# A Swin block on one core: K, Q and V as three fp16 products each, the loop written out, fc2 rows ahead of the first transposes

## The reference

```python
y = roll(ln(x, norm1_g, norm1_b), (-3, -3))        # then cut into 8 x 8 windows of 49 pixels
q, k, v = heads(yw @ qkv_w.T + qkv_b)              # 16 heads of 8 channels
attn = softmax(q * 8**-0.5 @ k.T + bias + mask)    # 49 x 49 for each window and head
o = roll(windows_back((attn @ v) @ proj_w.T + proj_b), (3, 3))
x = x + o
h = gelu(ln(x, norm2_g, norm2_b) @ fc1_w.T + fc1_b)   # 512 hidden channels
return x + (h @ fc2_w.T + fc2_b)
```

## Time and profile before

| | before |
|---|---|
| median of 3 runs | 4402.2 us (4398.3 to 4403.4) |
| the profiled execution | 4409.2 us, its span 4407.4 us |
| PE busy | 4134.3 us, 94% |
| weight loads (PEld) | 3265.2 us, 74% |
| DVE busy | 2743.0 us, 62% |
| ACT busy | 2889.0 us, 66% |
| POOL busy | 2014.4 us, 46% |
| mean granted TensorE clock | 0.983 of the upper level |
| row maxima, DVE line 576 | 1024 of 975 ns |
| exp, ACT line 418 | 1024 of 822 ns |
| K and Q, PE line 816 | 1024 records (two for each fp32 product) |
| V, PE line 850 | 4096 records |
| transfers | 443 MB, the 16 DMA engines 34% busy |

### The profile page before, as it was taken

One profiled execution on the slowest core, in us unless ns is written; L12 is line 12 of the kernel. 1 busy time (PEld: TensorE's weight loads), 2 busy tenths in 40 slices (PEclk: granted clock), 3 DMA queues, 4 the chain that ended last, 5 costly groups with the idle time before them and its releaser, 6 DMA issues.

```text
span 4407.4 us, 179808 instructions
## 1 busy us (share of the span) xinstructions
PE 4134.3 (94%) x72586; PEld 3265.2 (74%) x72586; DVE 2743.0 (62%) x6930; ACT 2889.0 (66%) x5120; POOL 2014.4 (46%) x3472
## 2 busy tenths in 40 slices
PE   3999999999999999999999999999999999999998
PEld 2777777777777777777777777777777777777777
DVE  5666665666656656566565656666566566666663
ACT  2666666666666666666666666766666666666665
POOL 4444444444444444444444444444444444444443
PEclk8999999999999999999999999999999999999999
DMA  2333333333333333333333333333333333333332
GB/s 77 102 106 102 98 105 97 105 102 98 105 99 104 109 95 101 98 105 102 99 104 97 105 101 99 105 101 102 94 105 105 99 104 107 104 104 105 106 106 62
DMA packets 626000, 443.34 MB, mean 101 GB/s; under 512 B 158451, under 2 KB 624611, under 8 KB 625059
## 3 DMA queue, kind: packets, MB, share of 16 engines
q1 hardware_dynamic: 624595, 428.82, 32.4%
q0 software_dynamic: 464, 1.81, 0.1%
HBM read 106.07 MB, written 51.46 MB: 36 GB/s over the span
## 4 chain that ended last, share of the span: by engine, by line
PE 82%; ACT 9%; issue 4%; DVE 3%; SPq 1%; DMA 0%; POOL 0%; ACTq 0%; POOLq 0%; DVEq 0%
PE ps L782 18%; PE ps L752 11%; PE ps L766 10%; PE ps L704 10%; PE ps L816 8%; PE ps L739 7%; PE ps L734 7%; PE ps L850 5%; PE ps L796 3%; DVE neg_max L576 2%; ACT L411 2%; ACT v_own L491 2%; PE ps L809 2%; ACT hid L435 2%; ACT probs L418 2%
## 5 line engine op out<-in xcount | busy, mean ns | idle before, releaser
L576 DVE TENSOR_REDUCE neg_max<-ps 113x16 f32<-113x784 f32 x1024 | 998.1, 975 | 514.5 <-PE ps L704 489.4
L418 ACT ACTIVATE probs<-ps 113x784 f32<-113x784 f32 x1024 | 841.1, 822 | 476.1 <-PE ps L739 470.5
L782 PEld LDWEIGHTS ps<-w,hid 128*112 128x112 f32 x7168 | 845.2, 181 | 49.7 <-issue 18.9
L782 PE MATMUL ps<-w,hid 128*112 128x128 f32 x7168 | 865.9, 277 | 0.0
L435 ACT ACTIVATE hid<-ps,col 128x448 f32<-128x448 f32 (+1 forms) x1024 | 541.6, 585 | 420.9 <-PE ps L766 417.8
L739 PE MATMUL ps<-st_q,st_k 128*49 128x196 f16 x8192 | 701.3, 250 | 4.2 <-issue 4.2
L734 PE MATMUL ps<-bias,eye_k 108*64 108x392 f16 x4096 | 686.6, 332 | 0.0
L752 PE MATMUL ps<-probs,v_own 113*32 113x49 f32 x32768 | 584.8, 211 | 101.0 <-issue 71.2
L752 PEld LDWEIGHTS ps<-probs,v_own 113*32 113x32 f32 x32768 | 438.4, 110 | 275.9 <-issue 245.7
L704 PE MATMUL ps<-mx_k,mx_q 128*49 128x196 f16 x8192 | 547.3, 254 | 20.6 <-DMA mx_k<-k_hi 9.3
L739 PEld LDWEIGHTS ps<-st_q,st_k 128*49 128x49 f16 x8192 | 447.0, 105 | 129.2 <-issue 7.1
(11 more groups left out here) (81 smaller groups left out, 6471.9 us busy)
## 6 DMA issues: line engine op xcount, KB each, us to landing
st_k<-k_hi SPq DMA_DIRECT2D x256, 196.0 KB
st_q<-q_hi SPq DMA_DIRECT2D x1024, 49.0 KB
oT_raw<-pv_sb SPq DMA_DIRECT2D x256, 196.0 KB, 2.6
x_in<-in_x SPq DMA_DIRECT2D x224, 196.0 KB
x_res<-in_x SPq DMA_DIRECT2D x224, 196.0 KB
out_y<-y_out SPq DMA_DIRECT2D x224, 196.0 KB
mx_q<-q_hi SPq DMA_DIRECT2D x128, 196.0 KB
mx_k<-k_hi SPq DMA_DIRECT2D x512, 49.0 KB
```

The costliest lines, as they stand in the source:

```text
L418: nc.scalar.activation(probs[0:KP, w % 2, :].rearrange("p (b c) -> p b c", b=2), ps[0:KP, b:b + 2, 0:HB * WT], ACT.Exp).then_inc(s_exp, 1)
L576: nc.vector.tensor_reduce(neg_max[0:KP, :, w, :], ps[0:KP, 0:2, 0:HB * WT].rearrange("p b (h k) -> p b h k", k=WT), AX_X, ALU.max, negate= ...
L782: last = mm(tokens_of(6)[0:TP, i, :], hid[:, c, i * TP:(i + 1) * TP], w_2[:, c, :], start=(c == 0), stop=(c == CH - 1))
```

## The change

**Loop.** `turns` becomes a plain loop in Python over all t, so that the program is written out in full; `apart` falls away, its waits stay, and all values are constants.

**Weights.** norm1's scale is multiplied into the weights of K, Q and V in the set-up, and its offset goes through three small products into the offsets. DVE splits each weight into a high and a low fp16 part. One more copy of V's weights is loaded for that, and POOL clears the four new tiles yT_hi and yT_lo.

**yT.** ACT copies without scale and offset, into a buffer that is also oT's. DVE makes two fp16 tiles of it: yT_hi, a copy, and yT_lo, what is left. Each holds for every window the two images side by side, 64 columns each (49 used).

**Products.** K and Q: high x high, low weight x high, high weight x low, of 392 columns each. V: for each window three products whose stationary operand are the 128 columns of both images.

**Order.** PE: fc2 rows 0 and 1 before the z1 transposes; rows 2 and 3 before K and Q; fc1 4 to 7 together, before V. ACT: all eight gelu, the table load for exp, then V's copies. DVE: reciprocal, yT_hi, yT_lo ahead of h_lo; V's second copy behind x1.

```diff
-UNROLL = 8
-LOOP_1 = (4, EDGE - 4)
...
-        def apart(eng, sem_, value):
-
-            eng.wait_ge(sem_, value)
-            eng.sem_inc(s_apart[eng.engine], 1)
...
+        def turns(body):
+            for t in range(-2, STEPS + 3):
+                body(t, lambda n: n >= EDGE, lambda k: (t + k) % 2)
...
-        yT = [sb(f"yT{e}", [C, 2, NW, WT]) for e in range(2)]
+        yT_hi, yT_lo = ([sb(f"{n}{e}", [C, NW, 2, HP], F16) for e in range(2)] for n in ("yT_hi", "yT_lo"))
...
+        yT = oT[:, :, :].rearrange("p i c -> p (i c)").rearrange("p (m w q) -> p m w q", m=2, w=NW)
...
+                nc.gpsimd.memset(yT_hi[e][:, :, :, :], 0.0)
+                nc.gpsimd.memset(yT_lo[e][:, :, :, :], 0.0)
...
-                    if past(n, 1):
-                        act.wait_ge(s_v, 2 * (n - 1))
+                    if past(n, 0):
+                        act.wait_ge(s_y_lo, n)
...
-                        return nc.scalar.activation(o, a, ACT.Identity, scale=col[:, G1:G1 + 1],
-                                                    bias=col[:, B1:B1 + 1])
+                        return nc.scalar.activation(o, a, ACT.Copy)
...
-                    for m in range(6):
+                    for m in range(2 * CH):
                         gelu(t - 2, m)
+                if exists(t):
+                    load_table(ACT.Exp)
...
-                if exists(t - 2):
-                    gelu(t - 2, 6)
-                    gelu(t - 2, 7)
                 if exists(t):
-                    load_table(ACT.Exp)
...
+            dve.wait_ge(s_inita, 2)
+            dve.wait_ge(s_w_split, 1)
+            then(nc.vector.tensor_tensor(col[:, BQ:BQ + 3], col[:, BQ:BQ + 3], ps[:, 7, 3 * C:3 * C + 3], ALU.add))
+            for ww, w_hi, w_lo in ((w_q, wq_hi, wq_lo), (w_k, wk_hi, wk_lo), (w_v, wv_hi, wv_lo)):
+                then(nc.vector.tensor_scalar(ww, ww, col[:, G1:G1 + 1], None, ALU.mult))
+                then(nc.vector.tensor_copy(w_hi[:, :], ww))
+                then(nc.vector.tensor_tensor(w_lo[:, :], ww, w_hi[:, :], ALU.subtract))
...
+                n = t - 1
+                if exists(n):
+
+                    dve.wait_ge(s_sum_dma, N_SUM * (n + 1))
+                    nc.vector.reciprocal(sums[:, :, :], sums[:, :, :]).then_inc(s_rsum, 1)
+                n = t + 1
+                if exists(n):
+
+                    dve.wait_ge(s_yT, n + 1)
+                    if past(n, 1):
+                        dve.wait_ge(s_v, 2 * (n - 1))
+                    if n < 2:
+                        dve.wait_ge(s_initp, 1)
+                    high, low = (y[odd(1)][:, :, :, 0:WT].rearrange("p w m q -> p m w q") for y in (yT_hi, yT_lo))
+                    flat = yT[:, :, :, :]
+                    nc.vector.tensor_copy(high, flat).then_inc(s_y_hi, 1)
+                    dve.wait_ge(s_y_hi, n + 1)
+                    nc.vector.tensor_tensor(low, flat, high, ALU.subtract).then_inc(s_y_lo, 1)
...
-                    for b in range(2):
-                        dve.wait_ge(s_v, 2 * n + b + 1)
-                        nc.vector.tensor_copy(v_place(0, b), v_made(0, b)).then_inc(s_vown, 1)
+                    dve.wait_ge(s_v, 2 * n + 1)
+                    nc.vector.tensor_copy(v_place(0, 0), v_made(0, 0)).then_inc(s_vown, 1)
...
+                n = t
+                if exists(n):
+                    dve.wait_ge(s_v, 2 * n + 2)
+                    nc.vector.tensor_copy(v_place(0, 1), v_made(0, 1)).then_inc(s_vown, 1)
...
+                if exists(t - 3):
+                    fc2(t - 3, 0, 2)
                 n = t + 1
                 if exists(n):
                     pe.wait_ge(s_z1, n + 1)
...
                     max_transposed(t)
-                if exists(t - 3):
-                    fc2(t - 3, 0, 2)
...
-                n = t + 1
-                if exists(n):
-                    pe.wait_ge(s_yT, n + 1)
-                    for wt, bank in ((w_k, 0), (w_q, 4)):
-                        for im in range(2):
-                            mm(ps[:, bank + im, 0:BT], wt[:, :], yT[odd(1)][:, im, :, :].rearrange("p w q -> p (w q)"),
-                               start=True, stop=True).then_inc(s_qk, 1)
                 if exists(t - 3):
                     fc2(t - 3, 2, 4)
+                n = t + 1
+                if exists(n):
+                    pe.wait_ge(s_y_hi, n + 1)
+                    high, low = ([y[odd(1)][:, :, im, 0:WT] for im in range(2)] for y in (yT_hi, yT_lo))
+                    for w_hi, w_lo, bank in ((wk_hi, wk_lo, 0), (wq_hi, wq_lo, 4)):
+                        for im in range(2):
+                            mm(ps[:, bank + im, 0:BT], w_hi[:, :], high[im], start=True, stop=False)
+                            mm(ps[:, bank + im, 0:BT], w_lo[:, :], high[im], start=False, stop=False)
+                        if bank == 0:
+                            pe.wait_ge(s_y_lo, n + 1)
+                        for im in range(2):
+                            mm(ps[:, bank + im, 0:BT], w_hi[:, :], low[im], start=False, stop=True).then_inc(s_qk, 1)
...
-                    fc1(t - 2, 4)
-                    fc1(t - 2, 5)
+                    for m in range(4, 2 * CH):
+                        fc1(t - 2, m)
...
-                            for im in range(2):
-                                last = mm(ps[HP * im:HP * im + WT, 6 + b, (w % 4) * C:(w % 4 + 1) * C],
-                                          yT[odd(0)][:, im, w, :], w_v[:, :], start=True, stop=True)
+                            for part, (yy, ww) in enumerate(((yT_hi, wv_hi), (yT_lo, wv_hi), (yT_hi, wv_lo))):
+                                last = mm(ps[:, 6 + b, (w % 4) * C:(w % 4 + 1) * C],
+                                          yy[odd(0)][:, w, :, :].rearrange("p m q -> p (m q)"), ww[:, :],
+                                          start=(part == 0), stop=(part == 2))
...
-                if exists(t - 2):
-                    fc1(t - 2, 6)
-                    fc1(t - 2, 7)
```

More of the change, by code:

```diff
@@ L138, in swin_block_kernel @@
         w_1, bv_wide = hid[:, 3, 0:HID], hid[:, 3, HID:HID + TP]
+        w_q, w_k, w_v, w_vp = (oT_raw[:, k // 3, (k % 3) * C:(k % 3 + 1) * C] for k in range(4))
         strips_k, strips_q = (nc.dram_tensor(n, [WS, NH, (2 * WS - 1) * WS], F32, kind="Internal").ap()
@@ L204, in band_dmas @@
                     eng.dma_start(d if store else s, s if store else d).then_inc(signal, 16)
-        def apart(eng, sem_, value):
-            eng.wait_ge(sem_, value)
-            eng.sem_inc(s_apart[eng.engine], 1)
[L211 to L221, removed]
+        def turns(body):
+            for t in range(-2, STEPS + 3):
+                body(t, lambda n: n >= EDGE, lambda k: (t + k) % 2)
+        N_W, N_CONST = 10, 7
         block = ctx.enter_context(nc.Block())
@@ L265, in body @@
                 n = t + 2
-                if exists(n) and not (isinstance(n, int) and n == 0):
+                if exists(n) and n != 0:
                     sp.wait_ge(s_t1, n)
@@ L500, in body @@
                             copy_pv(t, w - 1)
-            turns(act, body)
+            turns(body)
         @block.vector
@@ L566, in finish @@
                     if past(n, 0):
-                        dve.wait_ge(s_stored, loads(n - 1, edge(n) and (not isinstance(n, int) or edge(n - 1))))
+                        dve.wait_ge(s_stored, loads(n - 1, edge(n) and edge(n - 1)))
                 dve.wait_ge(s_fc2, 2 * n + p + 1)
@@ L668, in body @@
                             aggregate(n, st2, s_st2, mv2, s_ln2)
-            turns(dve, body)
+            turns(body)
         @block.tensor
@@ L680, in _ @@
                    start=True, stop=True)
+            pe.wait_ge(s_inita, 2)
+            for c, ww in enumerate((w_q, w_k, w_vp)):
+                last = mm(ps[:, 7, 3 * C + c:3 * C + c + 1], ww, col[:, B1:B1 + 1], start=True, stop=True)
+            last.then_inc(s_w_split, 1)
             pe.wait_ge(s_bv, 1)
-            mm(ps[0:TP, 7, 0:C], bv_wide[:, :], w_p[:, :], start=True, stop=True).then_inc(s_bp_mm, 1)
+            mm(ps[0:TP, 6, 0:C], bv_wide[:, :], w_p[:, :], start=True, stop=True).then_inc(s_bp_mm, 1)
             pe.wait_ge(s_inita, 2)
@@ L869, in body @@
                         max_logits(t + 1, w, edge)
-            turns(pe, body)
+            turns(body)
 def kernel(**inputs):
```

65 lines of the change are left out of this document (31 added, 34 removed).

## The result

| | before | changed |
|---|---|---|
| median | 4402.8 us (4398.3 to 4404.3, 4 runs) | 4175.3 us (4173.6 to 4179.8, 4 runs) |
| ratio | | 0.9486 (95%: 0.9470 to 0.9503) |
| span of the profiled execution | 4407.4 us | 4171.8 us |
| PE busy | 94% | 96% |
| DVE, ACT, POOL busy | 62%, 66%, 46% | 70%, 65%, 51% |

The change takes 227 us off; 173 were forecast (4230, range 4145 to 4320). The copy of the transposed maxima, now line 581, again counts the steps. The row shows the stretch that was looped before, to be held against the earlier trace rows.

The account below looks back on a forecast made before the run. PE, 94% busy and nearly without gaps, was taken as the bound, plus the loop's 1.40 us a step. Looped steps 172, tail 6, set-up -5 gave 173 us off 4409.2; with the median 7 lower, 4230 (4145 to 4320).

Parts of the forecast that it names:

- Part 1: Looped steps: written out, all 103 run like the 20 behind the loop, 1.40 us a step, 144 us off.
- Part 2: Products on PE in fp16: K and Q gain 0.67 us a step, V at 1.4 us gains 0.5.
- Rival (a): V's products on PE: weight loads show and V costs up to 2.6 us; 4380, half of that 4304; chance 0.10.
- Part 3: Chain from z1 transposes over yT to fc1: K/Q saving and 0.57 gap eaten by waits; second half starts 13.55.
- three new waits: PE around K, Q and fc1: waits for yT_hi 0.3, yT_lo 0.6 and Q's low parts 0.3, together 1.2 us.
- The gain of the gap: PE before the z1 transposes: fc2 rows moved ahead use the idle 0.57 us a step.
- Part 4: fc1's second half to second maximum product: V savings hidden by DVE and ACT; gain 0.28 us a step, period 32.17.
- rival (c): DVE's y_lo waits up to 2.1 us for POOL's x_res addition; period up to 2.6 longer, 4545 us; chance 0.08.
- rival (d): DVE pair costs less or waits overlap more; without the three waits period 31.3, 4120 us; chance 0.16.
- (b): Loop: writing out gives back only half of the 144 us, or nothing; 4302 to 4374 us; chance 0.08.
- the prediction's other signs: Profile: 32.2 us steps, no long issue waits, y_hi 0.68, y_lo 1.1, V 1.4, PE waits, second maximum product awaiting DVE.

Follow-up runs that it names:

- experiment 1: Kernel before with its loop written out, nothing else changed: 4289.1 us (0.974); also the changed kernel with the hardware loop put back: 4282.5 us (0.972).
- experiment 5: Changed kernel with ScalarE's copy to yT made as before, with scale and offset from columns: 4190.3 us (0.950).
- experiment 2: Kernel before, written out, fp32 products, with the change's fc2 order: 4219.7 us (0.959); with the second half's order added: 4235.3 us (0.961).
- Experiment 3: Changed kernel without 8 of V's 24 products: 4178.4 us (0.949); or without 4 of 12 K and Q products: 4172.7 us (0.946).
- experiment 7: Changed kernel with first exp before ACT's second V copy: 4165.5 us; plus DVE's first maximum before its V copy: 4203.1; early exp plus Q before K: 4123.2.

## Why the prediction was right, and where it was off

The forecast's sign, cause and order of size hold; the wide range held the time, its own narrower range (4195 to 4265) did not. It was 55 us too high. By the medians the loop gave 29 us less than forecast (115 for 144) and all the rest 84 more (113 for 29). That the two errors point opposite ways is luck, and it brings the forecast nearer than its parts are.

**Part 1, the loop: right in kind, 19 us too large in the steps.** 144 us were taken; experiment 1 shows 125 in the steps. The assumption that all straight code runs like the 20 steps behind the loop failed by 0.18 us a step: single supply gaps of up to about 1 us. That a part of the loop's cost is a fallen clock (experiment 1) the prediction didn't see; it read the page's slices, in which the clock is near its upper level.

**Part 2, the products: right.** The twelve products of K and Q would cost 2.04 us without waits (0.17 each; 1.98 forecast), V 1.34 (1.4 forecast). Rival (a) is out: 128 columns of load at every 128 columns of product run at 56 ns. So is the Trainium skill's 81 ns (TensorE: Matmul & The Clock Gate, Back-to-back issue gap) for this case.

**Part 3, the chain: right path, 0.51 us too long.** The prediction had three new waits, 1.2 us together. For yT_hi there was none (0.3 forecast), for yT_lo 0.26 in the step shown and 0.34 in the median step (0.6 forecast), for q_lo 0.32 (0.3 forecast). yT took 1.04 us, not 1.76 (experiment 5); a saving for the plain copy had been put at nothing. That alone would have moved yT_hi little, which stood behind the reciprocal. The two DVE operations were priced from the set-up, 683 and 1101 ns, in the very stretch in which the earlier trace rows show POOL at work. In the changed kernel's set-up the same two come when POOL has just ended (37.84 and 3.97 make 41.81), and they are shorter:

```profile
37.84 3.97 POOL L348 TENSOR_SCALAR x_in<-x_in,rs,nm 112x128 f32<-112x128 f32 x7
```

```profile
41.84 0.57 DVE L545 CAST hid<-hid 128x784 f16<-128x784 f32 x1
42.44 0.97 DVE L546 TENSOR_TENSOR hid<-hid 128x784 f16<-128x784 f32 x1
```

In the step, where DVE has begun before POOL's short operations come, the two take 509 and 979 ns. The steps of ACT's four high parts were taken as 0.6 us, but in the earlier trace rows each followed an fp32 product, and these come 0.66 apart; in the new kernel they take 0.51 (3918.21 to 3920.24 for four). The gain of the gap was booked as 0.57, and it is 0.6 (experiment 2).

**Part 4, the second half: right.** From fc1's second half to the first PV 6.95 us were forecast and 7.05 measured; PE's 0.3 us of wait for exp was 0.26. Experiment 3 shows what that means: behind a gate, PE at 96% busy does not gain from less work. From fc1's second half to the second maximum product 7.70 were forecast and 7.53 measured. The second V copy on DVE was forecast to be the last gate, at 0.75 us behind the first PV; the second maximum product came at 0.48 with no wait, and with exp out of the way it comes at 0.68 (experiment 7). DVE's copy and maximum take 0.94 to the next start and 0.93, not 1.05 and 0.97.

**Sums that don't come out.** fc1's 1.7 and V's 1.4 were added to 3.2 (16.75, by its own terms 16.65), while the 3.5 from V's end to the first PV is 3.66 in the kernel with exp early; the two nearly cancel. In rival (c) 2.6 x 123 gives 4550, not 4545. In rival (d) the three waits of 1.2 would give a period of 31.0, not 31.3.

**The sum by parts**, each kernel against the next one that ran: loop 115, fc2's order 69, the second half's order -16, products and what belongs to them 60. They make up the whole by construction. The prediction had 144 for the loop and 34 for all the rest, less 5 for the set-up. It said that most of the products' saving would be hidden, and it is: PE's work fell by 1.2 us a step (2.65 + 1.9 against 2.04 + 1.34), of which 60 us, 0.5 a step, arrive. The medians over more than 100 steps of the two traces show whose they are. From the z1 transposes to fc1's second half the kernel with fp32 products takes 11.25 us and the changed one 11.32; from there to the second maximum product 8.09 and 7.53; the rest of the step 12.70 and 12.72. So V's saving (0.55) arrives in full, because x1 and the second maximum product stood behind V, and that of K and Q (0.6) is eaten by the chain over yT.

**Rivals.** (b) is true for 0.18 us of 1.40. (c) did not come in: in the changed kernel POOL's x_res starts 0.7 us after yT_lo has ended, and POOL waits instead. Its mechanism exists, at a lower price than the up to 2.6 us a step that it was given: with x_res first it is 1.36 us a step, 176 us, and what is held is yT_hi. The Trainium skill (SBUF — State Buffer, SBUF: two separate sides) names DVE operations with two SBUF inputs or in a two-port mode; the 1.97 us cast has one input, so it agrees with the second if it runs in such a mode, which no run here shows by itself. (d), the better side, is what came in part: 4175 lies below the forecast's own range and halfway from 4230 to the 4120 of (d), and the step shown, 31.50, stands where the prediction put the mark for a wrong forecast (below 31.5), with the median step, 31.61, just above it. Of the prediction's other signs, yT_hi's wait and the wait of the second maximum product for DVE did not show.

## What to carry to other kernels

When an engine is nearly always busy, ask of each product what waits behind it: here leaving out 8 of 24 or 4 of 12 products gave nothing, while one reordering on three engines, with no work saved, gave 42 us. V's first saving did arrive, until exp became the gate. Take the price of an operation from a stretch where its neighbours are quiet, or note who was at work beside it: waiting can be inside the listed time. A hardware loop has a cost that can be read off before anything is changed, if some of the same steps also stand outside it; look at the granted clock there too, in stretches of a few microseconds.

## What the runs showed of the hardware that was not expected

In the looped kernel PE stood for some 6 us once in nearly every iteration of eight steps, and its clock was mostly at the lower level for 7 to 10 us there (13 stretches, 99 us in all); written out, neither was seen between set-up and end. DVE's cast from SBUF to SBUF (fp32 to fp16, 784 elements) takes 0.51 us when it is first and 1.97 us when POOL started a 2.08 us addition just before; POOL's subtraction of 98 elements takes 0.37 us before the change and 1.03 beside yT_lo. Products of 128 fp16 columns, each with a new stationary operand of 128 columns, follow each other every 56 ns. Straight code still loses about 0.2 us a step to gaps in PE's supply, most of them in the last four windows; what causes them stays open.
